# Graph layers on one core: the running maximum as the first value of the next chunk's sweep

## What is computed

```python
h = jnp.maximum(_layernorm(x), 0.0)
x = x + relu(matmul(matmul(support(adj), h), weight))        # layer 0
h = jnp.maximum(_layernorm(x), 0.0)
q = (h @ Wq.T).reshape(d, n, 8)                              # d = 128 score matrices, n = 3327
k = (h @ Wk.T).reshape(d, n, 8)
v = (h @ Wv.T).reshape(d, n, 8)
a = jnp.einsum('dnh,dmh->dnm', q, k) * scale
a = a + adj + adj
a = jax.nn.softmax(a, axis=2)                                # over the keys m
x = x + jnp.einsum('dnm,dmh->dnh', a, v).reshape(n, -1) @ Wo.T
```

## Time and profile before

| what | value |
|---|---|
| median of 3 runs | 14494.9 us (14490.62 to 14495.88) |
| profiled execution, its span | 14491.4 us |
| PE matmul busy | 13865.6 us (96%) |
| VectorE busy | 13834.8 us (95%) |
| ScalarE busy | 13501.7 us (93%) |
| GpSimd busy | 326.8 us (2%) |
| sweeps | 13312, 1047 ns each |
| accumulator reads | 13312, 140 ns each, partly beside the next sweep |
| reductions of the four chunks | 208, 253 ns each |

### The profile page before, as it was taken

One profiled execution on the slowest core, in us unless ns is written; L12 is line 12 of the kernel. 1 busy time (PEld: TensorE's weight loads), 2 busy tenths in 40 slices (PEclk: granted clock), 3 DMA queues, 4 the chain that ended last, 5 costly groups with the idle time before them and its releaser, 6 DMA issues. The chain is left out here.

```text
span 14491.4 us, 399097 instructions
## 1 busy us (share of the span) xinstructions
PE 13865.6 (96%) x145131; PEld 4680.7 (32%) x145131; DVE 13834.8 (95%) x27589; ACT 13501.7 (93%) x30466; POOL 326.8 (2%) x945
## 2 busy tenths in 40 slices
PE   3889999999999999999999999999999999999999
PEld 2533333333333333333333333333333333333334
DVE  4589999999999999999999999999999999999993
ACT  1269999999999999999999999999999999999997
POOL 1100000000000000000000000000000000000000
PEclk7989999999999999999999999999999999999999
DMA  8975655656565565656556565655556565565653
GB/s 277 258 161 134 142 135 133 143 134 142 135 143 135 133 144 134 142 135 143 134 133 144 135 142 135 142 135 135 141 135 142 135 142 134 135 141 134 142 134 97
DMA packets 2075116, 2082.15 MB, mean 144 GB/s; under 512 B 818905, under 2 KB 1827808, under 8 KB 2066752
## 3 DMA queue, kind: packets, MB, share of 16 engines
q1 hardware_dynamic: 2069118, 2043.41, 58.8%
q10 hardware_dynamic: 4032, 13.31, 0.2%
HBM read 1922.23 MB, written 133.76 MB: 142 GB/s over the span
## 5 line engine op out<-in xcount | busy, mean ns | idle before, releaser
L234 DVE CUSTOM_DVE_ANT_0 X<-X,adj_row 128x832 f32<-128x832 f32 x13312 | 13343.6, 1047 | 77.2 <-PE X L256 32.6
L1007 ACT ACTIVATE prob<-S 128x416 f32<-128x416 f32 x26624 | 11961.1, 519 | 236.1 <-PE S L1075 41.7
L1075 PE MATMUL S<-q_blk,k_res 52*128 52x416 f16 x26624 | 7026.2, 344 | 29.4 <-ACT S L996 8.4
L1096 PE MATMUL O<-prob,v_pad 128*32 128x208 f32 (+1 forms) x88752 | 6740.1, 385 | 2.6
L256 PE MATMUL X<-mk,mq 40*128 40x416 f16 x26624 | 6293.7, 343 | 260.7 <-DVE m_part L234 227.4
L1075 PEld LDWEIGHTS S<-q_blk,k_res 52*128 52x128 f16 x26624 | 2094.6, 93 | 4591.0 <-ACT prob L1007 1405.8
L1096 PEld LDWEIGHTS O<-prob,v_pad 128*32 128x32 f32 x88752 | 1860.1, 108 | 2507.3 <-issue 2022.4
L256 PEld LDWEIGHTS X<-mk,mq 40*128 40x128 f16 x26624 | 1507.2, 93 | 2267.2 <-DVE m_part L234 1547.8
L234 DVE DVE_READ_ACCUMULATOR2_ANT m_part<- 128x1 f32 x13312 | 1868.9, 140 | 0.0
L996 ACT ACTIVATE S<-adj_key 128x416 f32<-128x416 f32 x3328 | 1755.0, 527 | 35.4
L206 POOL TENSOR_SCALAR m_neg<-m_full 128x16 f32<-128x16 f32 x208 | 52.5, 253 | 13059.0 <-DVE m_full L217 13058.8
(11 more groups left out here) (86 smaller groups left out, 1044.8 us busy)
## 6 DMA issues: line engine op xcount, KB each, us to landing
adj_key<-adj_by_key SPq DMA_DIRECT2D x3328, 208.0 KB, 3.4
adj_row<-in_adj SPq DMA_DIRECT2D x1200, 416.0 KB, 3.8
mk<-k_planes SPq DMA_DIRECT2D x1664, 104.0 KB
adj_row<-adj_tail SPq DMA_DIRECT2D x400, 416.0 KB, 3.9
mk<-k_planes SPq DMA_DIRECT2D x1664, 52.0 KB
row<-in_adj SPq DMA_DIRECT2D x47, 1663.5 KB, 8.3
adj_by_key<-aT SPq DMA_DIRECT2D x26, 1664.0 KB, 11.8
q_planes<-q_parts SPq DMA_DIRECT2D x26, 1024.0 KB, 15.1
```

What stands on the lines that cost most here:

```text
L234: nc.vector.tensor_tensor_reduce(out=x_, in0=x_, in1=adj_row[gi % 4][:].rearrange("p (a b) -> p a b", a=2), scale=1.0, scalar=LOW, op0=ALU ...
L1007: nc.scalar.activation(prob[c % QR][:, d % 4, :], S[b][:, 0:WB], ACT.Exp, scale=2.0).then_inc(s_e[b], 1)
L1075: nc.tensor.matmul(S[b][:, 0:WB], k_res[base:base + KR, d // 2, s * P:(s + 1) * P], q_blk[n % 2][base:base + KR, d // 2, :], start=False, ...
L1096: done = nc.tensor.matmul(O[32 * d:32 * d + 32, cols], v_pad[:, s, 4 * q + d, :], prob[born(j, q) % QR][:, d, cols], start=first, stop=Tru ...
```

## The change

A sweep of chunk 0 keeps LOW as its first value. A sweep of chunk c > 0 takes as its first value the result that the sweep of the same head and tile left for chunk c - 1, a column of 128 x 1 in `m_part`. The column of chunk 3 then holds the maximum over all four chunks. `max_reduce` with its `tensor_reduce`, the tile `m_full` and the semaphore `s_mr` are gone; GpSimd reads `m_part[:, 3, :]` and waits on the 64th sweep of the block (`s_t`). Ahead of the first head of a chunk c > 0 there is a new wait on `s_t`, that the sweep nine units earlier is done.

```diff
 def max_planes(pool, xh, p):
-                wait(pool, s_mr, xh + 1)
-                nc.gpsimd.tensor_scalar(m_neg[:], m_full[p][:], -1.0 / MAX_STEP, None, ALU.mult).then_inc(s_pc, 1)
-                nc.gpsimd.tensor_scalar(m_pln[p][:, :, 0, :], m_full[p][:].rearrange("p (t d) -> p t d", t=2), -1.0 / MAX_STEP, None, ALU.mult).then_inc(s_pc, 1)
+                wait(pool, s_t, xh * 64 + 64)
+                nc.gpsimd.tensor_scalar(m_neg[:], m_part[p][:, 3, :], -1.0 / MAX_STEP, None, ALU.mult).then_inc(s_pc, 1)
+                nc.gpsimd.tensor_scalar(m_pln[p][:, :, 0, :], m_part[p][:, 3, :].rearrange("p (t d) -> p t d", t=2), -1.0 / MAX_STEP, None, ALU.mult).then_inc(s_pc, 1)
...
-            def max_reduce(dve, xh):
-
-                dve.wait_ge(s_t, xh * 64 + 64)
-                nc.vector.tensor_reduce(m_full[xh % 2][:], m_part[xh % 2][:].rearrange("p c a -> p a c"), AX.X, ALU.max).then_inc(s_mr, 1)
-
...
 def sweep(dve, v):
                 if d == 0:
                     dve.wait_ge(s_ar[gi % 4], xh * 32 + 16 * (gi // 4 + 1))
+                    if c:
+                        dve.wait_ge(s_t, v - 8)
                 dve.wait_ge(s_x[u % 2], xh * 32 + (u // 2 + 1))
                 x_ = X[u % 2][:, :, 0:XC]
+                at = GH * t + d
+                so_far = m_part[xh % 2][:, c - 1, at:at + 1] if c else LOW
                 nc.vector.tensor_tensor_reduce(out=x_, in0=x_, in1=adj_row[gi % 4][:].rearrange("p (a b) -> p a b", a=2),
-                                               scale=1.0, scalar=LOW, op0=ALU.add, op1=ALU.max,
-                                               accum_out=m_part[xh % 2][:, c, GH * t + d:GH * t + d + 1]).then_inc(s_t, 1)
-                if u == 1 and xh:
-                    max_reduce(dve, xh - 1)
+                                               scale=1.0, scalar=so_far, op0=ALU.add, op1=ALU.max,
+                                               accum_out=m_part[xh % 2][:, c, at:at + 1]).then_inc(s_t, 1)
```

More of the change, by code:

```diff
@@ L126, in graph_layers_kernel @@
             m_part = [sb(f"m_part{i}", [P, 4, 2 * GH], fp32) for i in range(2)]
-            m_full = [sb(f"m_full{i}", [P, 2 * GH], fp32) for i in range(2)]
             m_neg = sb("m_neg", [P, 2 * GH], fp32)
@@ L138, in graph_layers_kernel @@
             s_mp = sem("s_mp")
-            s_mr = sem("s_mr")
             s_tr = sem("s_tr")
@@ L1046, in _ @@
                             sweep(dve, v)
-                        max_reduce(dve, NG * XG - 1)
                         max_turn(dve, NG * XG - 1)
```

## The result

The changed kernel takes 14588.3 us (median of 4 runs, 14581.6 to 14590.4) against 14495.1 us before (median of 4): +93 us, a ratio of 1.0063 with a 95% interval from 1.0049 to 1.0078. It is slower, as forecast, but by 93 us and not by the forecast's 205: 14588 is almost exactly the lower end of the forecast's sum (14590), and not its middle.

The account below looks back on a forecast made before the run. The prediction saw a ring through PE's queue and ScalarE as the bound, VectorE just faster. From 14491.4 us, +207 (operand), -7 (reductions) and +3 (first stage) gave 14694, with 3.5 for the median 14698, rounded to 14700; range 14560 to 14870.

Parts of the forecast that it names:

- the lower end of the forecast's sum: Total time if the operand costs 32 ns per sweep and the period becomes 1.025 us: 14590 us.
- What bounds the kernel: Main stage: PE and ScalarE set the 1.015 us period; VectorE is 0.03 us per sweep faster.
- The ring of PE and ScalarE: Main stage: PE's in-order queue and ScalarE's key-bias copy hold up the next product, setting 1.015 us per sweep.
- The waits: 1248 added waits ahead of first sweeps of chunks 1 to 3: cost 0, or 26 us if not run ahead.
- The reduction: 208 reductions leave VectorE, 0.17 us each; most went into the margin, so about 0.035 us each, 7 us saved.
- The fetch: Sweeps of chunks 1 to 3 read a per-partition value from SBUF: 32 ns if half hidden, up to 62 ns.
- The period: Main-stage sweeps with the operand: 1.025 or 1.047 us, middle 1.036 taken against 1.015, +207 us over 9846 sweeps.
- My reason for the 1.025: At 32 ns VectorE needs 1.012 us, leaving 0.003 us margin instead of 0.035, so late sweeps cannot be caught up.
- free: Rival: the value is fetched while the previous sweep streams, leaving only a saving of 7 to 35 us; chance 0.10.
- absorbed: Rival: the price is 32 ns or less and the ring covers it, 0 to +40 us; chance 0.06.
- nothing absorbed: Rival: each of 9846 sweeps adds its full 62 ns to the period, +610 us, 15100 us; chance 0.05.
- the lost overlap: Rival: the fetch waits until the preceding accumulator read has written, +740 to +1330 us; chance 0.05.

Follow-up runs that it names:

- The run with 387 columns: The changed kernel with sweeps over 2 x 387 columns (58 left out, 60 ns less per sweep): 14453.6 us, ratio 0.9971.
- the second operand: The changed kernel with the factor 1.0 also read from an SBUF column in the sweeps of chunks 1 to 3: 14993.3 us, ratio 1.0346.

## Why the prediction was wrong

*What bounds the kernel*: right in that VectorE stands just below the pace and does not set it; shortening the sweeps by 33 and 133 ns brought 74 and 143 us instead of 433 and 1746. The ring of PE and ScalarE fits the waits, but no run tests it.

*The waits*: right, nothing (the kernel without the reductions takes 14480.8 us with them, and 14479.6 without them where GpSimd takes the reductions).

*The reduction*: 7 us taken, 12 measured (11 and 13 by way of GpSimd). The step that halved the 0.06 us between reduction and transpose gave too much to the transpose: without the reduction chunk 0 falls from 1.0192 to 1.0161 (1.0155 by way of GpSimd), 0.05 to 0.06 us in 16 sweeps. The interval is as wide as the difference.

*The fetch*: 62 ns was right (59 on late sweeps, 60 behind a copy, 60 and 62 for lines 602 and 622). Line 606, set beside line 615, is a different operation, so that comparison says nothing. Which end of "32 to 62 ns" holds behind an accumulator read was left open; it is the lower one, even a little below: 1.005 us between back-to-back sweeps for the 1.012 I had.

*The period*: this is the term that was mis-sized. The two ends gave 1.025 and 1.047, and "I take the middle, 1.036" is the step that failed: the measured period is 1.0255. 9846 x 0.0105 = 103 of the 112 us between 14700 and 14588; the rest are the reduction's 5 us and small terms. The middle was no mechanism of its own. The fetch either is covered or is not, so the sum should have gone to one end, and the forecast's time should have been 14590 or 14810. The trace had no instruction that reads an operand and uses the accumulator behind an accumulator read, so it could not say which. Both rows that I named for it (line 615 behind a read and behind a copy) were of an operation that never had the wait.

*My reason for the 1.025* is not borne out, and that the estimate comes within 0.001 of the measured period is in part luck. I argued from the margin of back-to-back sweeps, 0.003 us instead of 0.035, that late ones are no longer caught up. Measured, the changed kernel's period stands 0.02 us above its back-to-back sweep (1.0255 against 1.005). The run with 387 columns has a back-to-back sweep 37 ns shorter than the kernel before and the same period, so around the kernel before it isn't this margin that counts. My reading, which no run shows by itself, is that a late sweep stands in the ring, between PE's product and PE's next one, and pays the full 59 ns there: 0.011/0.059, about a fifth of it, reaches the period. In the changed kernel most of PE's waits for a sweep end with a back-to-back one, so there its 23 ns may count as well; which of the two prices makes the 0.011 us stays open.

*The rivals*: free is refuted by the lengths; absorbed had its price right behind an accumulator read (23 ns, under its 32), but its +40 us are too small, since 0.011 us per sweep still reach the period; nothing absorbed (15100 us) is refuted here, and for the second operand 42 of 62 ns reach the period; the lost overlap did not occur, the fetch behind an accumulator read costs less (23 ns), not more.

## What to carry to other kernels

An operand read per partition instead of a constant cost 60 ns on each VectorE instruction here, and 23 ns on a sweep directly behind an accumulator read; before an operation is saved in this way, compare how many instructions get the operand (9984) with how many operations go (208). Where several engines stand over 90%, shorten and lengthen the suspected one by known amounts: a gain of 143 us for 1746 us of work, and a loss of 106 us for the first 60 ns but 405 us for the second, tell where the bound lies better than any busy share. And where an unknown has two possible values, predict one of them and not their mean.

## What the hardware showed that I had not expected

- A sweep with an accumulator right behind an accumulator read needs about 40 ns more than behind a copy (982 against 940 ns to its own read), and the fetch of one operand runs inside this: 1005 against 1000 ns with the operand. A second operand finds no cover (1067 against 1060).
- With 133 ns less in each sweep the kernel gains 1.0%. A step then takes 1.005 us, PE's record is busy for 99% of the time and ScalarE's for 98%, and VectorE's for 91%: the step falls by about 10 ns for 133 ns less in each sweep.
